# Cross-attention and FFN on one core: the ScalarE table sets, the layer norm's place and the TensorE work around the maxima's transposes

## The reference

```python
def attention(q, k, v):                       # q = layernorm(x), k = v = ctx
    qh, kh = heads(q @ Wq.T), heads(k @ Wk.T)
    vh = heads(v @ Wv.T + bv)
    s = einsum('bhsd,bhtd->bhst', qh, kh) / sqrt(32)
    s = where(triu(ones, k=0) with [0, 0] allowed, -inf, s)   # strictly causal
    return merge(softmax(s) @ vh) @ Wo.T + bo

def ffn(x):                                   # x = layernorm(x)
    h = bitlinear(x, w_fc) + gate * (x @ v.T @ fast_b.T @ u.T)
    return bitlinear(relu(h) ** 2, w_proj)    # bitlinear: weights ternary times a row scale

x = x + attention(layernorm(x), ctx, ctx)
x = x + ffn(layernorm(x))
```

## Time and profile before

| | |
|---|---|
| Time, median of 3 runs | 2805.74 us (2803.74 to 2810.54) |
| Span of the profiled execution | 2803.6 us |
| Its busy shares | TensorE 95%, VectorE 60%, ScalarE 40%, GpSimd 13% |
| Attention setup | 0 to 47 us |
| Attention, 16 batches | 47 to 1655 us, 100 us each |
| FFN setup | 1655 to 1725 us |
| FFN, 16 batches | 1725 to 2803.6 us, 67 us each |

### The profile page before, as it was taken

How to read it: one execution, slowest core, us unless ns; L and a number is a source line. 1 busy time by engine, 2 the same in 40 slices (tenths; PEclk the granted TensorE clock), 3 DMA queues, 4 the chain that set the end, 5 groups by cost and what they waited for, 6 DMA issues and landing times. The chain is left out here.

```text
span 2803.6 us, 46166 instructions
## 1 busy us (share of the span) xinstructions
PE 2666.3 (95%) x15410; PEld 1979.3 (71%) x15410; DVE 1688.5 (60%) x3278; ACT 1111.7 (40%) x1965; POOL 377.6 (13%) x791
## 2 busy tenths in 40 slices
PE   7999999999999999999999967999999999999998
PEld 5666666667666666666766645888888888888887
DVE  4676766776767677677676666444444444444444
ACT  2533443443353344244335245444344334433332
POOL 1212121121121212112112110000000000000000
PEclk9999999999999999999999977999999999999999
DMA  4343253333334325333333332000000000000000
GB/s 129 84 112 99 61 135 92 81 98 98 88 85 114 97 62 134 90 79 103 98 85 88 96 104 76 30 30 30 30 30 30 30 30 30 30 30 30 30 30 31
DMA packets 116803, 198.81 MB, mean 71 GB/s; under 512 B 19987, under 2 KB 22035, under 8 KB 116260
## 3 DMA queue, kind: packets, MB, share of 16 engines
q1 hardware_dynamic: 116772, 198.42, 25.6%
HBM read 63.08 MB, written 33.55 MB: 34 GB/s over the span
## 5 line engine op out<-in xcount | busy, mean ns | idle before, releaser
L715 ACT ACTIVATE probs<-bank 128x512 f32<-128x512 f32 x640 | 369.2, 597 | 339.6 <-PE bank L529 329.6
L1125 PE MATMUL y_bank<-projT,a_hi 128*128 128x512 f32 x1024 | 409.1, 399 | 0.0
L1113 PE MATMUL h_bank<-x2T_hi,fcT 128*128 128x512 f32 x1024 | 406.2, 397 | 0.9 <-ACT scale_row L1196 0.9
L1114 PE MATMUL h_bank<-x2T_lo,fcT 128*128 128x512 f32 x1024 | 406.6, 397 | 0.0
L1127 PE MATMUL y_bank<-projT,a_lo 128*128 128x512 f32 x1024 | 403.9, 394 | 0.0
L1204 ACT ACTIVATE relu<-h_bank,scale_fc 128x512 f32<-128x512 f32 x256 | 176.0, 687 | 464.8 <-PE h_bank L1117 464.8
L464 POOL TENSOR_SCALAR_AFFINE_SELECT probs<-probs 128x256 f32<-128x256 f32 (+1 forms) x640 | 234.1, 366 | 872.7 <-ACT probs L715 870.1
L1314 DVE CAST a_hi<-act_sq 128x512 fp32r<-128x512 f32 x256 | 121.0, 472 | 373.6 <-ACT act_sq L1209 373.6
L529 PE MATMUL bank<-stack 98*128 98x512 f32 (+3 forms) x1024 | 286.0, 351 | 28.3 <-ACT probs L715 26.0
L504 PE MATMUL bank<-stack 96*128 96x512 f32 (+3 forms) x1024 | 266.0, 330 | 17.8 <-DVE maxima L777 11.8
L777 DVE TENSOR_REDUCE maxima<-bank 128x1 f32<-128x512 f32 x256 | 175.9, 687 | 162.2 <-PE bank L508 162.2
(11 more groups left out here) (182 smaller groups left out, 4623.9 us busy)
## 6 DMA issues: line engine op xcount, KB each, us to landing
stack<-stage SPq DMA_DIRECT2D x768, 128.0 KB, 2.3
x_in<-in_x_dram SPq DMA_DIRECT2D x16, 1024.0 KB, 5.3
x<-x_res SPq DMA_DIRECT2D x64, 256.0 KB, 2.4
x_in_sb<-x SPq DMA_DIRECT2D x16, 1024.0 KB, 5.6
out_dram<-y_sb SPq DMA_DIRECT2D x64, 256.0 KB, 2.0
xc_rows<-in_ctx_dram SPq DMA_DIRECT2D x15, 1024.0 KB, 5.2
stack<-m_stage SPq DMA_DIRECT2D x128, 8.0 KB, 1.8
w_nat<-in_L_ffn_w_fc_dram SPq DMA_DIRECT2D x2, 1024.0 KB, 6.7
```

What stands on the lines that cost most here:

```text
L715: act.activation(probs[:, s[2], :], t_bank[u % 2][:, :], ACT.Exp, scale=SCALE).then_inc(exp_done, 1)
L1113: pe.matmul(h_bank[b % 2][:, :], fcT[:, k, cols], xT_hi[:, k, :], start=k == 0, stop=False)
L1114: pe.matmul(h_bank[b % 2][:, :], fcT[:, k, cols], xT_lo[:, k, :], start=False, stop=False)
L1125: pe.matmul(y_bank[j][:, :], a_hi[:, b % RING, P * j:P * j + P], projT[:, b, :], start=b == 0, stop=False)
```

## The change

It has four parts.

1. `preload_act_table_set("natural_log_exp_and_others")` stands in front of each loop program of ScalarE. The built program then has 2 table loads where 8 stood (two in each setup and two in each loop body); the second stands at the end of the FFN setup.
2. The layer norm of the next batch is taken apart: its statistics stay where they were, ahead of T(1, 0) in ScalarE's and VectorE's lists. Its ScalarE piece stands behind T(1, 3). The Newton step and the LN_APPLYs stand four score and T units later, behind S(2, 2).
3. As the new steps count as units of the weave, the thirds of Q(3) and K(3) fall at other places.
4. XT(1) is done ahead of M(2), XT(2) and XT(3) move up by one place, Q(0) ends ahead of M(3) and the two CTs follow M(3).

```diff
 def setup_steps():
-    return ([("LN_STATS", j) for j in range(4)] + [("LN_VAR",)] + w(0) + [("LN_RSTD",)]
+    return ([("LN_STATS", j) for j in range(4)] + [("LN_VAR",), ("LN_RSTD",)] + w(0) + [("LN_NEWTON",)]
...
 def batch_steps(more):
-    layernorm = ([("LN_STATS", j) for j in range(4)] + [("LN_VAR",), ("LN_RSTD",)]
-                 + [("LN_APPLY", j) for j in range(4)])
+    stats = [("LN_STATS", j) for j in range(4)] + [("LN_VAR",)]
+    apply = [("LN_NEWTON",)] + [("LN_APPLY", j) for j in range(4)]
...
-    steps += v3[0:2] + [("M", 1), ("STACK", 2, 1)] + v3[2:] + pv(0) + nxt(*layernorm)
+    steps += v3[0:2] + [("M", 1), ("STACK", 2, 1)] + v3[2:] + nxt(*stats) + pv(0)
 
     t1 = with_copy(1, 6)
-    steps += weave(t1[:4] + weave(score("S", 2), t1[4:]), parts("Q", 3) + parts("K", 3) + [("STACK", 3, 0)], rest=4)
-    steps += nxt(("XT", 0)) + [("M", 2), ("STACK", 3, 1)] + weave(norm(0)[:4], pv(1)[:2])
-    steps += [("NM", 0, 0)] + nxt(("XT", 1)) + [("NH", 0, 0), ("NL", 0, 0)] + pv(1)[2:]
+    s2_t1 = weave(score("S", 2), t1[4:])
+    steps += weave(t1[:4] + nxt(("LN_RSTD",)) + s2_t1[:4] + nxt(*apply) + s2_t1[4:],
+                   parts("Q", 3) + parts("K", 3) + [("STACK", 3, 0)], rest=4)
+    steps += nxt(("XT", 0), ("XT", 1)) + [("M", 2), ("STACK", 3, 1)] + weave(norm(0)[:4], pv(1)[:2])
+    steps += [("NM", 0, 0)] + nxt(("XT", 2)) + [("NH", 0, 0), ("NL", 0, 0)] + pv(1)[2:]
 
     t2, ct = with_copy(2, 6), nxt(("CT", 2), ("CT", 3))
-    steps += weave(t2[:2], nxt(("XT", 2), ("XT", 3))) + nxt(("C_LOAD",))
-    steps += weave(weave(score("S", 3), t2[2:]), (parts("Q", 0) if more else []) + ct[:1], rest=2)
-    steps += ct[1:] + [("M", 3)] + pv(2) + norm(1)
+    steps += t2[:1] + nxt(("XT", 3)) + t2[1:2] + nxt(("C_LOAD",))
+    steps += weave(weave(score("S", 3), t2[2:]), parts("Q", 0)[:2] if more else [], rest=2)
+    steps += nxt(("Q", 0)) + [("M", 3)] + ct + pv(2) + norm(1)
...
+            act.preload_act_table_set("natural_log_exp_and_others")
             in_loop(act, program)
```

More of the change, by code:

```diff
@@ L147, in is_next @@
 def is_next(step, in_batch):
-    return in_batch and (step[0] in ("LN_STATS", "LN_VAR", "LN_RSTD", "LN_APPLY", "XT", "CT")
+    return in_batch and (step[0] in ("LN_STATS", "LN_VAR", "LN_RSTD", "LN_NEWTON", "LN_APPLY", "XT", "CT")
                          or step[:2] in (("Q", 0), ("K", 0), ("STACK", 0)) or step[:3] == ("PART", "Q", 0))
@@ L708, in program @@
                         act.activation(bias_sb[:, :], out[:, :], ACT.Copy).then_inc(mm_hi, 1)
-                    elif s[0] == "LN_VAR":
+                    elif s[0] == "LN_RSTD":
                         act.wait_ge(var_ready, b + 1)
@@ L792, in program @@
                         ln_var(dve, chain, ln, TT, dve_passed).then_inc(var_ready, 1)
-                    elif s[0] == "LN_RSTD":
+                    elif s[0] == "LN_NEWTON":
                         dve.wait_ge(rstd_ready, b + 1)
```

## The result

The changed kernel takes 2847.47 us (median, 2846.45 to 2848.97), the kernel before, run beside it, 2806.38 us (2803.74 to 2810.54). The ratio is 1.0144, with a 95% interval of 1.0129 to 1.0158: slower by 1.4%. The forecast was 2839 us.

What follows compares the result with a forecast made beforehand. TensorE bounds the kernel, idle nearly 4 us per attention batch; VectorE's order decides. Terms 1.03 + 0.13 + 1.0 + 0.15 = 2.3 us a batch, times 15, less 1 in setups: 2839 us, 8-in-10 range 2800 to 2855.

Steps and rivals of the forecast that it cites:

- Table loads: Attention loop: T(1,2) follows T(1,0) by 1.19 us instead of 1.75, -0.56 us a batch (bounds 0 and 1.00).
- the FFN: FFN loop: removing its table loads gains nothing, since TensorE is busy throughout and does not wait.
- VectorE's half of the norm: Group 2: Newton step and LN_APPLYs between the reductions of S(2,2) and S(2,3) cost 1.36 us, then net +0.24, a batch.
- the stall: TensorE at S(2,5): waits 1.36 us a batch for the reduction of S(2,3), bounds 0 and 1.6.
- S(2,8) and S(2,9): Late group 2: they wait some 0.40 and 0.52 us for the reductions of S(2,6) and S(2,7).
- The nested rival: Rival: S(2,5)'s wait lets VectorE catch up, so later stalls don't appear; 3 us in all, 2808 us; chance 0.10.
- Around M(2): From M(2) to S(3,2): S(3,2) waits 0.69 us instead of 0.44 for S(3,0)'s reduction, about +0.13 net a batch.
- Group 3 and CT(3): Group 3 waits at S(3,3), S(3,7) and trifles, +1.0 us; CT(3) waits about 1.0 for Q(0)'s bank, net +0.15.
- The sum: Whole kernel: 2.3 us a batch times 15, +34.7, less 1 in the setups, +33.7; span about 2837, median 2839 us.
- The FFN setup: First layer norm of the FFN setup: VectorE's wait for the exponential shrinks, -0.8 us once (bounds 0 and -2.6).
- The signs: Profile after: two loads, reduction waits over 3 us a batch, CT(3) waiting 0.7 to 1.0, batch of 102.2 us.
- The faster rival: Rival: VectorE finishes the LN_APPLYs before S(2,5) is wanted and all removed waits count; -26 us, 2780; chance 0.12.

Runs made afterwards that it cites:

- the tables alone: Kernel before with the activation table set loaded once ahead of both loops and nothing else changed; 2791.6 us, ratio 0.996.
- the loads put back: Changed kernel without its two preload lines, so the compiler again puts in a load ahead of the log and of the exponential; 2849.8 us, ratio 1.015.
- VectorE's half alone: Kernel before with the table set loaded once and, in VectorE's list only, Newton step and LN_APPLYs behind the reduction of S(2,2); 2830.76 us, ratio 1.0075.
- one filler: Kernel before with the table set loaded once and the first third of Q(3) ahead of T(1,2); 2784.58 us, ratio 0.9922.
- the LN_APPLYs spread: Changed kernel, in VectorE's list one LN_APPLY behind each reduction of S(2,3) to S(2,6) instead of four ahead of the first; 2833.28 us, ratio 1.0113.
- the maxima's DMA first: Kernel with tables loaded once, XT(1) ahead of M(2) and Q(3)'s first third ahead of T(1,2), STACK(3,0)'s DMA issues moved behind M(2)'s; 2841.47 us, ratio 1.0126.

## Why the prediction was right, step by step

The direction and the mechanism were right, the size was short by 8.5 us (2839 for 2847.5, in the range). The forecast had 2.3 us a batch, and in the two batches laid side by side T(1,0) to PV(2) takes 32.32 us before (590.12 to 622.44) and 35.37 after (606.45 to 641.82), 3.05 more.

- **Table loads.** T(1,2) behind T(1,0): forecast 1.19, measured 1.19. But from T(1,0) to S(2,2) the batch gains 0.30 (4.89 for 5.19), not 0.56. The tables' term isn't what failed: with the tables alone the same stretch takes 4.63 us (586.29 to 590.92), 0.56 less. What I overlooked is the new weave. Before, the first third of Q(3) stands between T(1,2) and T(1,3); after the change T(1,3) follows T(1,2) at once and waits for T(1,1)'s exponential, so that from T(1,2) to the first product matmul it takes 0.82 us (607.64 to 608.46), where I had gone on with 0.57. Missed: 0.26 us. The experiment with the loads put back adds that the gain is not the tables' own in this version. For the FFN, 0 was forecast and 0 measured.
- **VectorE's half of the norm.** From S(2,2) to S(2,5) 5.45 us forecast, 5.49 measured; the stall 1.24 idle, or 1.40 in starts over the 0.23 of two products (1.36 forecast). This is the largest term of the change, and the experiment with VectorE's half alone shows it by itself: 1.60 us a batch, 24 us, and with the falls of the clock that came with it 39. S(2,8) and S(2,9) wait, start to start, 0.42 and 0.50 (0.40 and 0.52 forecast). From S(2,5) to M(2) it takes 0.18 more than laid out, for eight transposes in a row. The nested rival is refuted: the later waits do appear behind the long one.
- **Around M(2).** Not seen: PV(1) has a new wait of 0.35 on GpSimd's selection. S(3,2) waits 0.28 us where I had 0.69. From the first transpose of XT(0) to PV(1) it takes 1.50 us in both traces: where M(2) waited before, XT(1) is done now, and what is left of that time is PV(1)'s wait. It changes the place of a term more than the sum: from M(2) to S(3,2) 8.30 forecast (8.53 before), 8.26 measured.
- **Group 3 and CT(3).** S(3,3) and S(3,7) wait, start to start, 0.56 and 0.30 (0.57 and 0.30 forecast); CT(3) has the forecast idle time, 1.02 (about 1.0), M(3) none. Yet S(3,2) to PV(2) takes 10.91 us for a forecast of 10.6 (9.46 before, by the earlier trace rows). Up to M(3) it fits: without the two CTs that were in it, and without M(3)'s wait, this part took 7.60 us before and takes 8.60 now, the forecast +1.0. The fault is behind it. The two CTs, M(3) and all waits there took 1.86 us before and take 2.31 now (639.51 to 641.82), 0.45 more for a forecast 0.15. I had let the gap between the transposes and PV(2) go, and it is still there: CT(3) to PV(2) takes 0.59 us, where four transposes ahead of a T or S unit take 0.36 in the same trace. And CT(3)'s wait, start to start, is 1.25 us. Missed: 0.3 us.
- **The sum.** 0.26 + 0.04 + 0.18 - 0.04 + 0.3 = 0.74 us is what 3.05 has over 2.3, and would be 11 us over fifteen batches; the span is 9.4 over the forecast's 2837. The difference is one fall of the granted clock less than in the run before, 1.7 us, which the working didn't hold. The FFN setup gave back 1.2 (0.8 forecast). The prediction's own figures are a little loose in two places: 0.40 + 0.52 - 0.55 - 0.1 make +0.27 and not +0.24, and from 0.44 to 0.69 at S(3,2) it is 0.25, of which +0.13 was booked without saying why.
- **The signs.** One of those named came out short: TensorE's waits on the reductions are 2.85 us a batch (42.8 in fifteen), not over 3. The others came, the wait of CT(3) at the end of its 0.7 to 1.0 and the batch at 102.9 us for 102.2.
- **The faster rival** turned on whether the reduction of S(2,3) ends within 4.1 us of the start of S(2,2). It ends at 616.77, 5.43 us behind 611.34; 5.4 was laid out.

The gain that the change seemed to offer existed: of its four parts the first alone, the tables, with one filler that the change doesn't have, gives 0.8% instead of the loss of 1.4%.

## What to carry to other kernels

An engine that works in order and is idle 40% of the time can still have no room at a given place: lay out in starts what stands between two of its releases and when the engine that waits wants the second, and move its work only to where that comes out positive, here ahead of the first reduction of a group. A wait that is filled is worth only what the next chain behind it has to spare (0.65 us a batch at T(1,2), nothing at M(2)), so look up that chain (here SyncE's queue and a DMA) before booking the gain. And where work goes to a place at which its engine idles, the overhead around it, such as a table load here, costs nothing already.

## What the runs showed of the hardware

Batches of one kernel aren't all alike. Most last the same to 0.1 us, and a few 1.6 us more; the granted clock falls in them. In the profiled runs the attention phase has five such falls in the kernel before, four in the changed one, two with the tables alone, eight with the LN_APPLYs spread, and one in each of the first fifteen batches with VectorE's half alone. In that last kernel, two stretches of 4 us of one batch (us, busy times of the five engines with their counts, then the granted clock, the last but two):

```profile
742.90:746.90 4.00, 3.81 (x12) 2.81 (x12) 0.08 (x1) 2.68 (x6) 2.03 (x6) 0.72 0.00 0
746.90:750.90 4.00, 4.00 (x17) 2.94 (x17) 0.00 (x0) 2.80 (x6) 1.51 (x4) 0.86 0.00 0
```

And in the kernel with the maxima's DMA first, around the wait of S(3,0):

```profile
721.30:725.30 4.00, 1.15 (x9) 0.71 (x7) 1.62 (x4) 1.25 (x3) 0.64 (x2) 1.00 0.86 198
725.30:729.30 4.00, 3.86 (x15) 2.94 (x15) 2.45 (x6) 1.19 (x2) 0.70 (x2) 0.65 0.87 177
729.30:733.30 4.00, 4.00 (x21) 3.01 (x21) 2.61 (x6) 2.77 (x5) 0.94 (x3) 0.92 0.55 210
```

The granted clock is 1.00 (the level of 2.4 GHz) up to the wait, and right behind it 0.65 and 0.92 as a mean of 4 us, so for a part of the time it was at the level of 1.2 GHz. The matmuls of a product start 0.43 us apart there instead of 0.23 (726.93 to 727.36 in this trace). By the two clock figures that batch loses 4 x 0.35 + 4 x 0.08 = 1.7 us beyond the wait itself. In the kernel with VectorE's half alone the fall comes behind the short waits of T(3,2) and T(3,4), 0.45 and 0.19 us, which the changed kernel has too without a fall in most of its batches. What decides there whether the clock falls, and how the wait at S(2,5) 30 us earlier bears on it, stays open: it was not tried by itself. So a kernel with a longer stall can lose more than the stall's own length, and two executions of one kernel can differ by some us through the number of such falls, as the four of VectorE's half alone did.
